# Root products of the graph convolutions moved from the dense stage into the gather pass

## The reference

```python
def _graph_conv(x, src, dst, W_rel, b, W_root):
    agg = jax.ops.segment_sum(x[src], dst, num_segments=N)
    return agg @ W_rel + b + x @ W_root
...
h = jax.nn.elu(_graph_conv(x, src, dst, W1_rel, b1, W1_root))
h = jax.nn.elu(_graph_conv(h, src, dst, W2_rel, b2, W2_root))
h = jax.nn.elu(_graph_conv(h, src, dst, W3_rel, b3, W3_root))
```

## Time and profile before

| | |
|---|---|
| median of 3 runs | 8514.61 us (8514.19 to 8517.21) |
| profiled execution | 8526.32 us, span 8524.8 us |
| mean granted TensorE clock | 0.774 |
| PE busy | 4971.6 us (58%) |
| DVE busy | 3858.8 us (45%) |
| ACT busy | 1000.6 us (12%) |
| POOL busy | 5503.3 us (65%) |
| gathers of one convolution (L1567) | 784, 742.2 us busy |
| product of one dense stage (L2279) | 400 records, 95.9 us busy |

### The profile page before, as it was taken

How to read it: one execution, slowest core, us unless ns; L and a number is a source line. 1 busy time by engine, 2 the same in 40 slices (tenths; PEclk the granted TensorE clock), 3 DMA queues, 4 the chain that set the end, 5 groups by cost and what they waited for, 6 DMA issues and landing times. The chain is left out here.

```text
span 8524.8 us, 83297 instructions
## 1 busy us (share of the span) xinstructions
PE 4971.6 (58%) x17596; PEld 3833.7 (45%) x17597; DVE 3858.8 (45%) x6827; ACT 1000.6 (12%) x2667; POOL 5503.3 (65%) x5858
## 2 busy tenths in 40 slices
PE   4455564555553566675666756667465666455554
PEld 3344453344442445564445644456344544344443
DVE  5566675666664222242222422225422227466666
ACT  2000003000012000030000300002233333100003
POOL 5777745777724777747777377774577760677770
PEclk8677786777776777887778877888777887777776
DMA  5444424444424333333333333333333333544442
GB/s 176 130 118 117 117 72 122 117 117 118 117 72 127 105 105 105 100 107 105 105 105 105 103 105 105 105 105 105 120 105 105 105 100 111 147 118 120 118 118 66
DMA packets 450980, 942.69 MB, mean 111 GB/s; under 512 B 116799, under 2 KB 254331, under 8 KB 450178
## 3 DMA queue, kind: packets, MB, share of 16 engines
q0 software_dynamic: 277184, 753.08, 32.0%
q1 hardware_dynamic: 149997, 171.21, 6.5%
q10 hardware_dynamic: 23584, 16.32, 0.7%
HBM read 869.40 MB, written 77.99 MB: 111 GB/s over the span
## 5 line engine op out<-in xcount | busy, mean ns | idle before, releaser
L1567 POOL DMA_INDIRECT l1aa_messages<-table,l1aa_index x784 | 742.2, 947 | 464.4 <-issue 238.6
L1567 POOL DMA_INDIRECT l2a_messages<-table,l2a_index x784 | 742.3, 947 | 278.0 <-issue 238.6
L1567 POOL DMA_INDIRECT l1ba_messages<-table,l1ba_index x784 | 742.2, 947 | 248.9 <-issue 238.6
L1567 POOL DMA_INDIRECT l1ca_messages<-table,l1ca_index x784 | 742.3, 947 | 248.6 <-issue 238.6
L1205 POOL DMA_INDIRECT l3a_messages<-table_h,l3a_index x782 | 746.0, 954 | 238.3 <-issue 236.5
L1205 POOL DMA_INDIRECT l0aa_messages<-table_h,l0aa_index x782 | 745.2, 953 | 238.3 <-issue 237.7
L1205 POOL DMA_INDIRECT l0ba_messages<-table_h,l0ba_index x782 | 745.0, 953 | 238.3 <-issue 238.0
L1680 PE MATMUL l1aa_sums<-l1aa_messages,l1aa_member 128*128 x1952 | 609.6, 483 | 485.2 <-SPq L1576 478.1
L1680 PE MATMUL l2a_sums<-l2a_messages,l2a_member 128*128 x1952 | 607.4, 481 | 421.2 <-ACT l2a_messages L1615 413.4
L1680 PE MATMUL l1ba_sums<-l1ba_messages,l1ba_member 128*128 x1952 | 608.0, 482 | 393.6 <-SPq L1576 389.0
L1680 PE MATMUL l1ca_sums<-l1ca_messages,l1ca_member 128*128 x1952 | 601.7, 478 | 399.4 <-SPq L1576 390.0
(11 more groups left out here) (628 smaller groups left out, 6867.1 us busy)
## 6 DMA issues: line engine op xcount, KB each, us to landing
table<-l_acc SPq DMA_DIRECT2D x10, 1280.0 KB
l2b_xin<-table SPq DMA_DIRECT2D x100, 128.0 KB, 2.0
l1aa_messages<-table,l1aa_index POOLq DMA_INDIRECT x784, 2.7
l1ba_messages<-table,l1ba_index POOLq DMA_INDIRECT x784, 2.7
l1ca_messages<-table,l1ca_index POOLq DMA_INDIRECT x784, 2.7
l2a_messages<-table,l2a_index POOLq DMA_INDIRECT x784, 2.7
l0aa_messages<-table_h,l0aa_index POOLq DMA_INDIRECT x782, 2.8
l0ba_messages<-table_h,l0ba_index POOLq DMA_INDIRECT x782, 2.8
```

The lines of the kernel that those rows point to most:

```text
L1567: pool.indirect_dma_start(out=ring4[:, g % ROUND, j, 0:D], out_offset=None, in_=table, in_offset=bass.IndirectOffsetOnAxis(ap=index[:, g * ...
```

## The change

`sum_messages_phase` gets an argument `root` with the root weights, the bias, a DRAM table `root_dram` and `row_stats`. With it, the first 50 of the 122 units each also handle one row tile t. TensorE transposes the tile's 128 rows of x between the two steps of the unit (`turn_root`) and multiplies them by the root weights behind it (`multiply_root`). ScalarE copies the transposed rows from PSUM, stores the result of tile t-1 in `root_dram`, waits for that store, and loads the rows of tile t+1. VectorE adds the bias (`add_root`) between `add` and `begin`. The rows have two slots, one in `k.att` and one new; the transposed rows lie in `row_stats`; the bias lies in the padding tile of `acc`, loaded after `acc` is cleared. The eighth PSUM bank holds the transposes and the product.

`graph_conv_phase` loses the transposes of x, the root half of the product, the bias and the copy `place`. TensorE transposes straight out of `acc`, its loop is unrolled, and its first two transposes stand ahead of the wait for the weights (`w_in`, now 32). SyncE loads `root_dram` tiles instead of x, and VectorE's first operation adds them. The passes without `root` keep their order.

```diff
+            def root_tile(t, s, first, last):
+                act.wait_ge(root_turned, t + 1)
+                if not first:
+                    act.wait_ge(root_summed, t)
+                act.copy(xT, root_ps[:, 0:D]).then_inc(xT_made, 1)
+                if not first:
+                    act.wait_ge(root_added, t)
+                    act.dma_start(root_dram[bass.ds((t - 1) * P, P), :], (row_1, row_0)[s]).then_inc(root_stored, 16)
+                    if not last:
+                        act.wait_ge(root_stored, t * 16)
+                        act.dma_start((row_1, row_0)[s], table[bass.ds((t + 1) * P, P), :]).then_inc(loaded[1 - s], 16)
+            if root is not None:
+                for s in range(2):
+                    act.dma_start((row_0, row_1)[s], table[s * P:(s + 1) * P, :]).then_inc(loaded[s], 16)
+                for c in range(2):
+                    act.dma_start(w_sb[:, c, :], w_root[c * P:(c + 1) * P, :]).then_inc(w_in, 16)
+                act.wait_ge(acc_cleared, 1)
+                act.dma_start(bias_sb, bias.partition_broadcast(P)).then_inc(bias_in, 16)
...
+            def add_root(t, s):
+                dve.wait_ge(root_summed, t + 1)
+                dve.tensor_tensor((row_0, row_1)[s], root_ps[:, D:2 * D], bias_sb, ALU.add).then_inc(root_added, 1)
...
+                with dve.Fori(0, NTP // 6) as i:
+                    for s in range(6):
+                        add(i * 2 + s // 3, s % 3)
+                        add_root(i * 6 + s, s % 2)
+                        begin(i * 2 + s // 3 + 1, s % 3)
...
                     ins.then_inc(step_summed, 1)
+                    if r == 0 and between is not None:
+                        between()
+            def turn_root(t, s):
+                pe.wait_ge(loaded[s], (t - s) * 8 + 16)
+                if not before(t, 1):
+                    pe.wait_ge(root_added, t)
+                for c in range(2):
+                    ins = pe.transpose(root_ps[:, c * P:(c + 1) * P], (row_0, row_1)[s][:, c * P:(c + 1) * P], k.ident[:])
+                ins.then_inc(root_turned, 1)
+            def multiply_root(t):
+                pe.wait_ge(xT_made, t + 1)
+                for c in range(2):
+                    ins = pe.matmul(root_ps[:, D:2 * D], xT[:, c * P:(c + 1) * P], w_sb[:, c, :], start=(c == 0), stop=(c == 1))
+                ins.then_inc(root_summed, 1)
...
-def graph_conv_phase(nc, k, name, acc, table_in, w_rel, w_root, bias, table_out, residual, row_stats):
+def graph_conv_phase(nc, k, name, acc, root_dram, w_rel, table_out, residual, row_stats):
...
-            pipeline(act, (place, 0), (take, 1), (exp, 3))
+            pipeline(act, (take, 0), (exp, 2))
...
-            pe.wait_ge(w_in, 80)
...
-            pipeline(pe, (turn, 0), (multiply, 2), slots=4)
+            turn(0)
+            turn(1)
+            pe.wait_ge(w_in, 32)
+            for t in range(NTP):
+                multiply(t)
+                if t + 2 < NTP:
+                    turn(t + 2)
...
-            dve.wait_ge(w_in, 80)
...
                 dve.wait_ge(summed, t + 1)
+                dve.wait_ge(loaded[s], (t - s) * 4 + 16)
                 if not before(t, 2):
                     dve.wait_ge(y_made, t - 1)
-                dve.tensor_tensor(y[:, b, :], y_ps[b][:, 0:D], bias_sb[:], ALU.add).then_inc(y_summed, 1)
+                dve.tensor_tensor(y[:, b, :], y_ps[b][:, 0:D], root[:, s, :], ALU.add).then_inc(y_summed, 1)
```

More of the change, by code:

```diff
@@ L1555, in sum_messages_phase @@
         step_summed, step_added = m.sem("step_summed"), m.sem("step_added")
+        if root is not None:
+            w_root, bias, root_dram, row_stats = root
+            w_sb = m.sb("w_root", [P, 2, D])
+            row_0, row_1 = k.att[:, 0:D], m.sb("row_1", [P, D])[:]
+            xT = row_stats[:].rearrange("p t n -> p (t n)")[:, 0:D]
+            root_ps = m.ps("root_ps", [P, BANK])
+            bias_sb = acc[:, NT * MSGW:NT * MSGW + D]
+            w_in, bias_in, acc_cleared, root_stored = (m.sem(n) for n in ("w_in", "bias_in", "acc_cleared", "root_stored"))
+            loaded = [m.sem(f"loaded{s}") for s in range(2)]
+            root_turned, xT_made, root_summed, root_added = (
+                m.sem(n) for n in ("root_turned", "xT_made", "root_summed", "root_added"))
         block = ctx.enter_context(nc.Block())
@@ L1682, in sum_unit, with root_unit @@
                     ins.then_inc(step_summed, 1)
[L1684 to L1686 removed]
+                    if r == 0 and between is not None:
[12 more added lines that the diff above has]
+                ins.then_inc(root_summed, 1)
+            def root_unit(u):
+                sum_unit(u // 3, u % 3, u < 3, lambda: turn_root(u, u % 2))
+                multiply_root(u)
+            done = 1
+            if root is None:
+                for s in range(3):
+                    sum_unit(0, s, True)
+            else:
+                pe.wait_ge(w_in, 32)
+                for u in range(6):
+                    root_unit(u)
+                with pe.Fori(1, NTP // 6) as i:
+                    for s in range(6):
+                        sum_unit(i * 2 + s // 3, s % 3, False, lambda: turn_root(i * 6 + s, s % 2))
+                        multiply_root(i * 6 + s)
+                for u in range(NTP // 6 * 6, -(-NTP // 6) * 6):
+                    if u < NTP:
+                        root_unit(u)
+                    else:
+                        sum_unit(u // 3, u % 3, False)
+                done = -(-NTP // 6) * 2
+            with pe.Fori(done, units // 3) as i:
                 for s in range(3):
@@ L2226, in _ @@
         def _(sp):
[L2227 to L2230, removed]
+            for c in range(2):
+                sp.dma_start(w_sb[:, c, :], w_rel[c * P:(c + 1) * P, :]).then_inc(w_in, 16)
             def load(t, s, first):
                 if not first:
-                    sp.wait_ge(turned, t - 3)
-                sp.dma_start(xin[:, s, :], table_in[bass.ds(t * P, P), :]).then_inc(loaded[s], 16)
+                    sp.wait_ge(y_summed, t - 3)
+                sp.dma_start(root[:, s, :], root_dram[bass.ds(t * P, P), :]).then_inc(loaded[s], 16)
             pipeline(sp, (load, 0), slots=4)
```

88 lines of the change are left out of this document (51 added, 37 removed).

## The result

| | before | after |
|---|---|---|
| median of 4 runs each, us | 8514.4 (8513.5 to 8517.2) | 8442.0 (8438.6 to 8444.5) |
| ratio | | 0.9914 (0.9901 to 0.9926) |
| profiled execution, us (span) | 8526.3 (8524.8) | 8444.5 (8443.0) |

The kernel is faster by 72.4 us at the median; 8441 had been predicted. The two profiled executions differ by 81.8 us, because that of before lies 11.7 above its median and that of after 2.5. For a profiled execution 8453 us had been predicted, and 8444.5 came.

The account below looks back on a forecast made before the run. GpSimd was taken to bound gather passes, TensorE the first two dense stages, VectorE the third. Gains of 27.7 + 26.9 + 24 less 3 and 2.4 made 73.2 us: 8514.6 to 8441 us, range 8424 to 8478.

Parts of the forecast that it names:

- The sum: Whole kernel: gains of 27.7, 26.9 and 24 less 3 and 2.4 make 73.2 us, a median of 8441 us.
- The bound and the wait behind it: Dense tiles: VectorE sets the pace at 1.60 us; gains 27.7 and 26.9 us in two stages, third 0.
- half-clock tiles: First tiles of the first two dense stages: TensorE still at half clock, 1.5 us given back in each, 3 us.
- signs named: Expected in the profile if right: unchanged passes, dense periods 1.6, 1.6, 2.32 us, VectorE not waiting for TensorE, clock 1.00.
- The starts: Start of each dense stage: VectorE begins sooner, with fewer weights and less work first; 7.4, 8.0, 8.6, together 24 us.
- The index loads: Start of each gather pass: ScalarE's loads delay SyncE's index load, 0.8 us a pass, 2.4 us given back.
- The passes: Gather passes: root work on TensorE, ScalarE and VectorE hides behind GpSimd's gathers, costed at nothing.
- the case of lost cover: Gather pass: from about 12 us per unit, each further microsecond costs 50 us in each of three passes.
- Rival A: Dense stages: TensorE's clock falls in the shorter tiles; 8490 us, or 8466 if it swings; chance 0.13.
- B: Dense stages: something else holds the tile period near 2.16 us, only the starts gain; 8493 us, chance 0.08.
- C: Gather passes: the first 370 gathers take 1.01 instead of 0.947 us, costing 70 us; 8511, no change; chance 0.05.
- D: Gather passes: ScalarE's chain of copy, store, wait and load makes units too long; 8591 us at 13 us; chance 0.05.

Follow-up runs that it names:

- e4: The change with the subtraction of 1 folded into neighbouring operations, one VectorE operation less per dense tile; 8395.0 us, ratio 0.985 to the kernel before.
- e6: The change with each dense tile's product made twice, on a slower chip; 10586.5 us beside 10570.1 for the kernel before, ratio 1.0014.
- e1: The kernel before with the root work added in the gather passes, its dense stages left as they were; 8524.6 us, ratio 1.0005 to the kernel before.
- e5: The change itself, unedited, on a slower chip; 10540.3 us beside 10570.1 for the kernel before, ratio 0.9976.
- e12: The kernel before, unedited, profiled on a slower chip; 10624.4 us in its profiled execution.
- e8: The change with each unit's root product in the gather pass made 15 times, on a slower chip; 11441.0 us, ratio 1.0828 to the kernel before.

## Why the prediction was right

**The sum.** The median came within 1 us of the forecast, and part of that is luck. By the profiles the dense stages gave 79.4 us where 27.7 + 26.9 + 24 - 3 = 75.6 had been forecast, and the passes gave some 2 us where 2.4 were to be paid: 81.5 us against 73.2. At the medians it is 72.4, with 63 to 84 by the interval of the ratio. The mechanism held stage by stage; the last few us of the sum are not confirmed by it.

**The bound and the wait behind it.** VectorE had been named as what is late next, with a floor of 1.48 to 1.69 us from the unrolled end of the stage; 1.626 and 1.584 were measured against 1.60. With the half-clock tiles in it, the two stages gave 54.1 us against 54.6 - 3. The third gave 1.3 us against 0 plus or minus 2. e4 and e6 show this step from both sides: less on VectorE shortens the tile at once, more on TensorE only after about 0.45 us. The 1.60 itself was chosen between 1.48 and 1.69, and no row of before showed it. Two of the signs named were not clean: VectorE still waited for TensorE 11 times in the first stage, and the granted clock of the third was 0.90 to 0.96 and not 1.00.

**The starts.** 7.5, 8.1 and 8.4 us against 7.4, 8.0 and 8.6. The weights landed after 2.6 us instead of the 3.0 taken, and the product at half clock took 2.07 instead of 1.75. Two small misses cancelled.

**The index loads.** From index load to first gather it took 3.83, 3.89 and 3.80 us (3717.06 - 3713.17 is the second) against 3.30, 3.75 and 3.42 before: 1.05 us in three, where 2.4 had been taken and 0 to 6.6 were the ends. ScalarE's first loads of rows and weights landed in 4.1 to 4.4 us, where later row loads take 2.3, so both sides share the time, as the Trainium skill's page "DMA: Bandwidth & Descriptors", section "Issuing engines are not separate DMA queues", has it; the trace agrees in kind, with 0.35 us a pass for it.

**The passes.** The cost of nothing holds on the first chips (e1). TensorE's busy time grew by 0.57 us a unit and not by 1.1 to 2.1, as the clock rose with the added work. e5 to e12 show what that term rested on: where TensorE's side holds up the gathers, the same work costs 14 to 24 us a pass. The prediction had the case of lost cover in its text but put its point at 12 us a unit, since it counted the whole ring as free; there it lay near 10.

**Rival A** had the largest chance of the rivals, and fell. Stretches of after (columns as above), first stage, then second, then the third:

```profile
3660.00:3705.00 45.00, 34.17 (x155) 24.43 (x153) 37.54 (x112) 19.57 (x54) 15.51 (x28) 0.99 0.52 155
4718.00:4790.00 72.00, 58.61 (x266) 42.24 (x264) 61.65 (x184) 32.31 (x90) 24.98 (x46) 1.00 0.54 163
...
5850.00:5911.00 61.00, 37.12 (x146) 26.46 (x146) 54.96 (x159) 18.03 (x50) 13.54 (x25) 0.90 0.35 107
```

With weight loads busy for 24.4 of 45 us and a wait in nearly every tile, the granted clock is 0.99 to 1.00. The Trainium skill's page "TensorE: Matmul & The Clock Gate", section "A second HAM failure mode: psum-queue depth-cycling", warned of such micro-idles; in the first two stages the trace doesn't agree with it. In the third, where TensorE waits 42 times for 39.0 us in all, the clock does fall, to 0.90 on average, and costs nothing, since VectorE sets the pace, as the prediction had it for that stage.

**Rivals B, C and D.** The period fell (against B), the gathers kept 945 ns (against C), and TensorE waited 2.0 us for the rows of l1aa (against D).

## What to carry to other kernels

Read what is late next before counting what is saved: the tile gave 0.55 us and not the 1.05 that TensorE saved, and one operation of 0.29 us on the engine behind it was then worth 47 us. Work moved beside a stage that another engine paces is free only as long as that stage keeps its slack; measure the part alone (e1) and the cover by adding to it. On the slower chips added work began to cost at the period of a unit, about 10 us, and not at that period plus what the ring could hold. A gain made of covered work can be smaller on another chip than a gain made of work taken away: of 78 us in the dense stages 43 to 72 were given back there.

## What was not expected of the hardware

- Added work in a pass raised the granted clock (0.75 to 0.84), and 302 more records cost 28 us of busy time, where 302 records of e8's length would take 302 x 0.213 = 64.
- Three chips ran the same kernel before in 10570 to 10607 instead of 8515 us, with the dense stages unchanged to 1.2 us. In e5's passes TensorE, VectorE and ScalarE stand for 10 to 27 us between operations that depend on each other, for the first 200 us above all. In e12 there are also gaps between TensorE's own matmuls: it waited 645.7 us in 321 pieces for nothing that the profile shows, where in the trace of before it waited 478.1 us in 87 pieces for the relay, and at 3504.35, 3506.47 and 3509.26 us single matmuls of 0.58 us start. So the engines are late with their own instructions too, and not only with each other's results. The cause stays open.
